# TensorE's loop over local attention units announces its closing branch at the top of each turn

## What is computed

```python
def attn_layer(x, Wqkv, qs, ksc, Wo):
    q, k, v = jnp.split(x @ Wqkv, 3, -1)          # 16 heads of 64
    q = l2norm(q) * qs ; k = l2norm(k) * ksc
    q = q * cos * scale + rotate_half(q) * sin * scale
    k = k * cos * inv + rotate_half(k) * sin * inv
    out = local_attention(q, k, v)                # window 32, looks one window back
    return out.transpose(0, 2, 1, 3).reshape(b, n, INNER) @ Wo
```

## Time and profile before

| | |
|---|---|
| median of 3 runs | 3956.47 us (3954.7 to 3961.85) |
| profiled execution: its own time | 3953.85 us |
| its span, first to last instruction | 3951.3 us |
| granted clock of TensorE, mean over the span | 0.971 |
| TensorE matmul, busy | 3664.5 us (93%) |
| VectorE, busy | 3153.5 us (80%) |
| ScalarE, busy | 2880.3 us (73%) |
| GpSimd, busy | 2434.8 us (62%) |
| instructions on TensorE | 70910 matmuls, 70910 weight loads |
| DMA queue 8, instructions | 96 packets, 1.57 MB |
| DMA queue 14, instructions | 85 packets, 0.70 MB |

### The profile page before, as it was taken

One profiled execution on the slowest core, in us unless ns is written; L12 is line 12 of the kernel. 1 busy time (PEld: TensorE's weight loads), 2 busy tenths in 40 slices (PEclk: granted clock), 3 DMA queues, 4 the chain that ended last, 5 costly groups with the idle time before them and its releaser, 6 DMA issues. The chain is left out here.

```text
span 3951.3 us, 189393 instructions
## 1 busy us (share of the span) xinstructions
PE 3664.5 (93%) x70910; PEld 2927.3 (74%) x70910; DVE 3153.5 (80%) x9439; ACT 2880.3 (73%) x8501; POOL 2434.8 (62%) x2538
## 2 busy tenths in 40 slices
PE   5769999989999899999999999999999998699997
PEld 3448888678887788876888768888688885366665
DVE  5778888778887788877888878888788886566667
ACT  4647888578886688866888758888578884477775
POOL 3537777477774677756777557776477771354553
PEclk8879999999999999999999999999999999799998
DMA  1013333233332233332333323333233331100000
GB/s 41 6 35 82 81 80 80 63 79 80 80 80 77 67 80 81 80 82 59 81 80 79 92 51 79 81 80 79 65 79 80 81 81 26 36 1 0 0 0 27
DMA packets 305289, 245.99 MB, mean 62 GB/s; under 512 B 74485, under 2 KB 299860, under 8 KB 304340
## 3 DMA queue, kind: packets, MB, share of 16 engines
q1 hardware_dynamic: 305108, 243.72, 24.4%
HBM read 24.54 MB, written 2.12 MB: 7 GB/s over the span
## 5 line engine op out<-in xcount | busy, mean ns | idle before, releaser
L1172 POOL TENSOR_TENSOR wa_t<-wa_t,wa_rn 128x512 f32<-128x512 f32 x768 | 785.2, 1043 | 277.0 <-DVE wa_rn L1000 273.7
L825 ACT ACTIVATE wa_pb<-wa_sc,wa_nm 128x64 f32<-128x64 f32 x3072 | 670.1, 329 | 351.6 <-DVE wa_nm L1022 345.9
L1178 POOL TENSOR_TENSOR wa_t<-wa_t 128x512 f32<-128x512 f32 x384 | 496.3, 1292 | 440.4 <-DVE wa_t L976 440.2
L974 DVE TENSOR_TENSOR wa_t<-wa_pj,wa_ctab 128x512 f32<-128x512 f32 x768 | 527.4, 687 | 238.6 <-PE wa_ta L578 192.7
L44 PE MATMUL wa_pj<-lw_wqkv_high,wa_xhigh 128*128 128x512 f32 x1152 | 532.5, 462 | 79.3 <-issue 43.4
L808 ACT ACTIVATE wa_sq<-wa_pj 128x512 f32<-128x512 f32 x768 | 484.8, 633 | 104.1 <-PE wa_pj L46 102.6
L1187 POOL TENSOR_TENSOR wa_t<-wa_t 128x512 f32<-128x512 f32 x384 | 490.6, 1278 | 0.0
L46 PE MATMUL wa_pj<-lw_wqkv_high,wa_xlow 128*128 128x512 f32 x1152 | 461.1, 400 | 0.0
L45 PE MATMUL wa_pj<-lw_wqkv_low,wa_xhigh 128*128 128x512 f32 x1152 | 458.2, 398 | 0.0
L982 DVE TENSOR_REDUCE wa_raw<-wa_sq 128x16 f32<-128x1024 f32 x384 | 449.3, 1170 | 0.0
L646 PE MATMUL wa_ob<-wa_oT,wa_wo 128*128 128x128 f32 x3120 | 416.3, 276 | 1.0 <-DVE wa_on L1034 0.9
(11 more groups left out here) (285 smaller groups left out, 8611.8 us busy)
## 6 DMA issues: line engine op xcount, KB each, us to landing
wa_vv<-wa_vt SPq DMA_DIRECT2D x2304, 65.0 KB
wa_vv<-wa_vt SPq DMA_DIRECT2D x1152, 32.5 KB
lw_wqkv<-L_ffn_Wqkv SPq DMA_DIRECT2D x6, 1536.0 KB
lw_xs<-yT SPq DMA_DIRECT2D x96, 64.0 KB, 1.9
lw_fs<-yT SPq DMA_DIRECT2D x48, 128.0 KB
lw_xs<-yT SPq DMA_DIRECT2D x96, 63.8 KB, 2.0
lw_fs<-yT SPq DMA_DIRECT2D x96, 63.8 KB
wa_wo<-L_ffn_Wo SPq DMA_DIRECT2D x6, 512.0 KB, 4.0
```

The source lines that it names most:

```text
L825: last = nc.scalar.activation(pb[:, u.par(2), p, e, :], SC[:, e, p * KEYS:(p + 1) * KEYS], ACT.Exp, bias=nm[:, u.par(2), e, p:p + 1])
L974: nc.vector.tensor_tensor(t1[:, b, j], x, table(ctab, slice(0, HD)), ALU.mult)
L1172: nc.gpsimd.tensor_tensor(here, here, rn[:, u.par(1), j * HG:(j + 1) * HG].unsqueeze(2).broadcast_to((128, HG, HD)), ALU.mult).then_inc(s. ...
L1178: nc.gpsimd.tensor_tensor(t1[:, b, 0], t1[:, b, 0], t2[:, b, 0], ALU.add).then_inc(s.qadd_done, 1)
```

## The change

The loop of line 767 is opened with a hint. The body, its order and the number of turns are the same. [...]

```diff
--- before.py
+++ after.py
@@ -764,7 +764,7 @@
                     slot(Slot(layer, 2, 0))
                     pe.wait_ge(s.w_o, layer * 16 + 16)
                     slot(Slot(layer, 3, 0))
-                    with pe.Fori(0, NB - 1) as loop:
+                    with nc.Fori(0, NB - 1, engines=[pe.engine], hint_back_edge=True) as loop:
                         for k in range(UPS):
                             slot(Slot(layer, k, 1, loop))
                     first = LayerGroup(layer, 0)
```

## The result

The changed kernel takes 3976.87 us in the median of 5 runs (3975.68 to 3980.65), the kernel before 3956.47 us (3954.7 to 3961.85, 5 runs beside it). The ratio is 1.005, with a 95% interval of 1.0035 to 1.0064. I had forecast 3964.5 us and a range up to 3972.5: the sign holds, the size doesn't, and the time lies outside the range.

The account below looks back on a forecast made before the run. TensorE, busy for 93% of the span, was taken as the bound. Hint +8.0 us, branch 0 and code fetches 0 sum to +8.0 us on the median of 3956.47: 3964.5 us, range 3956 to 3972.5.

Parts of the forecast that it names:

- The bound: TensorE bounds line 767's loop, idle only 0.38 us at each turn's top; its closing branches don't miss their code.
- Part 1 and 2: Hint at line 767's turn tops: 0.09 us in each of 90 turns, nearly all in the period, taken as 8.0 us.
- The share of 94%: Share of a sequencer step's time at line 767's turn top that lengthens the period: 0.106 of 0.113 us.
- Part 3: Line 767's closing branch: the hint makes a taken branch no cheaper than 208 ns, so 0.
- rival A: Line 767's hinted taken branch costs 76 ns instead of 208: -3 us in all, 3953.5; chance 0.05.
- Part 4: Code fetches in a layer's first turn: waits move by one or two instructions, 0 within 1 us.
- rival C: At line 767's exits the following block wasn't fetched: 6 x 3.3 = 20 us atop the 8, 3984; chance 0.04.
- D: Hint refetches its target each turn of line 767, driving out needed code: 283 us atop the 8, 4248; chance 0.02.
- Rival B: Each taken branch of line 767 misses its code and the hint cures it: 283 us less, 3681; chance 0.01.

Follow-up runs that it names:

- after: The changed kernel, with the hint at the top of each turn of line 767, against the kernel before: 3976.87 us, ratio 1.005.
- the semaphore step: Kernel before plus a semaphore increment nobody waits for at the top of each turn of line 767, no hint: 3961.13 us, ratio 1.0024.
- outer: Kernel before plus a hint on the loop over layers, line 793, and none on line 767: 3957.73 us, ratio 1.0002.

## Why the prediction was wrong

**The bound.** Right. TensorE is the bound in the loop, it is idle only at the turn tops, and closing branches don't miss their code: in after they take 221 ns in the median, and queue 8 fetches nothing in the later turns.

**Part 1 and 2, the hint in the loop: 8.0 us.** Right in size, 7.8. Over 14 turns it was +2.3 us in the first layer, +1.3, +1.8, +1.1 and +1.3 in the next four, and 0.0 in the last, where the idle time of nine turns rose from 2.4 to 3.5 us and the nine turns only from 238.49 to 238.76. The share of 94% that I took from comparing the last layer with the others is too even: a step costs 0.11 us in a steady turn of the second layer and 0.03 in one of the last, for the hint and for the semaphore step alike (26.53 us a turn in both). Why the last layer takes it up is open. My reason, that it costs because nothing is queued there, was too simple: it cost about the same, 0.12 us a turn, with eight transposes queued.

**Part 3, the branch.** Right: 221 ns against 208, no gain; rival A falls. The 13 ns more aren't clearly the hint's, since the run outer has 222 ns on this branch without one.

**Part 4, fetches of new code: "0, within 1 us".** This step failed. It asked only where the existing waits for code would shift, and not whether the hint would change which code is fetched. In its place the runs showed 13.7 us of waits for code and some 16.5 us of time, over five exits. That question was in rival C, at about the right price (6 x 3.3 = 20 us). What failed was its chance of 0.04, and with it two readings:

- The reason given against C: "the hinted loop's exit took 80 ns, and TensorE's only wait in the 9 us behind it is for VectorE, 0.8 us". True, but the fetch that stood only behind that exit wasn't late for TensorE, by my account because the exit has room in its block. The absence of a wait at one place says nothing about another place at a different distance from the block's end.
- The reason given against D: "six hinted turns, no queue moved a packet". I read this only as a sign that the hint drives no code out. The window ended at the exit. A fetch stood 1.0 us behind it, and none had stood in the turns: that is the very mechanism, and a window 3 us longer shows it. In line 767's loop without a hint the last fetch starts ahead of the first closing branch, and the next only 3.4 us behind the exit.

With C at the price of a hinted exit whose block ends soon, the sum would have been 8 + 5 x 3.3 = 24.5 us: 3981, against 3976.87 measured.

**A miss at each taken branch.** Rival B falls: the loop's body has 1400 instructions, over five blocks, and its branches took 208 to 228 ns in the median of every run; none that closed a turn took more than 255. What was late was the code behind the exit, where the branch is not taken.

Open remains why the fetch behind a hinted exit starts 1.7 us after the branch in layers 1 and 5 (waits of 1.9 and 1.6 us) and 3.4 to 3.8 us after it in layers 2 to 4 (3.3 to 3.6 us). From the start of that fetch to the first matmul behind it there are 2.4 to 2.8 us in all five. Nor does any run show the reason for which an announced branch leaves the next block unfetched; they show only that it does.

## What to carry to other kernels

Before announcing a branch, look at its duration in the profile: in this kernel some 210 ns was a branch whose target is there, 3351 to 3882 ns one that misses. Only the second had anything to gain (3584 to 342 ns), and even that came back as waits for VectorE (11.0 us gone, 10.4 new). An announced branch that was not taken in the end left the code behind it unfetched, for 1.6 to 3.7 us of waiting at an exit; see what follows the loop and how far the block goes on (with some 250 instructions left in it, nothing waited). In this loop a sequencer step at the top of a turn cost 0.03 to 0.12 us each time, and moving the closing branch ahead of a group of long matmuls was worth more here (0.5%) than anything done to the branch.

## What the runs showed of the hardware that I had not expected

- A hint that says "taken" moved one 16 KB fetch (256 instructions) from just ahead of the first closing branch to 1.7 to 3.8 us behind the exit; one that was to say "not taken", from a register, left all fetches where they were.
- A hint on a branch that misses brought it from 3584 to 342 ns, over a body of a whole layer with unannounced loops inside.
- A wait of 3.3 us for code can cost clock as well: behind the second layer's exit the 3.5 us after it were granted 0.56 of the full clock, and seven matmuls of line 646 took 1.65 us where eight had taken 1.06; behind the fourth layer's, after as long a wait, it was 1.00.
- Placing the loop's head at slot 140 of its block made the kernel 0.45% slower without any other change: where the blocks' ends fall mattered here nearly as much as the hint did (0.5%).
